# Attention over 16 heads on one core: one accumulation bank instead of two, four banks instead of three for the row maxima, one chunk per slot

## The chip, the cores and the metric

The kernel runs on one NeuronCore of a Trainium2 chip. The metric is the device time of one execution in microseconds (us), lower is better. The time given for a kernel is the median of its runs.

## The reference, cut to what matters

A macaron layer: half a gated feed-forward, causal attention, half a gated feed-forward, each on a layer norm of its input. 2048 tokens of width 512, 16 heads of width 32. Only the attention is touched here:

```python
scores = einsum('bhqd,bhkd->bhqk', q, k) / sqrt(32)
scores = scores + triu(full((S, S), -inf), k=1)      # S = 2048
attn = softmax(scores, axis=-1)
out = einsum('bhqk,bhkd->bhqd', attn, v)
return einsum('bsd,ed->bse', out, w_out) + b_out
```

All is float32, and the weights of the attention are scaled up, so the softmax needs its true row maximum.

## The kernel before

`build` (L1468) runs `ffn`, `attend`, `ffn`. `attend` runs `project_in` (queries, keys and values into DRAM; in its last steps also the row maxima of head 0), `attention`, and `project_out`. PSUM has 8 banks of 128 x 512 float32.

**Two sweeps over the scores of each head.** The first finds the row maxima, with queries on the partitions: a *chunk* (`max_chunk`, L705) is a matmul of 128 queries by up to 512 keys into one of the banks 4 to 6, and `take_max` (L729) on VectorE reduces it to one maximum a row; a chunk on the diagonal (L744) adds the mask in the same instruction. When the last chunk of a block of 512 queries is in, `split_max` (L748, three small VectorE instructions, L751, L756, L758) negates the maximum and splits it into a high and a low part. `rows` (L719) then transposes these with four small matmuls into a bank of the same ring, and `store_rows` (L761) on ScalarE copies the two rows into the query tile. The second sweep has keys on the partitions: `scores` (L1195) multiplies 98 rows, the last two being the maxima, into one of the banks 0 to 2; for a tile on the diagonal VectorE adds the mask of its first 128 columns (`mask`, L1250); `exps` (L1280) on ScalarE writes the exponential to SBUF; `with_values` (L1212) multiplies it by the values and a column of ones.

**Blocks, tiles, lanes.** A head has query blocks 0 to 3 with 4, 8, 12 and 16 key tiles: 40 tiles, and 40 chunks as well. The tiles (`TILES`, L583) alternate between two lanes, lane 0 with block 3 and then block 0 on output partitions 0 to 32, lane 1 with block 2 and then block 1 on partitions 64 to 96. A float32 matmul with values is two instructions, and those of the two lanes run at the same time. Blocks 3 and 2 are summed in bank 3, blocks 0 and 1 in bank 7 (`BANKS`, L592). Block 2's last tile is tile 23, block 3's is 30, block 0's 38 and block 1's 39. ScalarE copies a bank out (`take_out`, L1291) after tiles 30 and 39, and SyncE stores the copies.

**Slots, written out by hand.** A head is 40 slots, and each engine goes through them in program order. In slot t, `head` (L1226) on TensorE issues the scores of tile t + 4 (of the next head from slot 36 on), the chunks of the **next** head that `chunks_of_slot(t)` gives, and the row transposes if t is in `ROWS_AT`. After every fourth slot come the four `with_values` of these slots (a *batch*: slots 0 to 3 are batch 0, 36 to 39 batch 9). The chunks are packed into slots 0 to 35, with two in slots 0, 9, 18 and 27 and none in 36 to 39; maxima are split in slots 13, 24, 31 and 35, and transposed four slots later, in the middle or at the end of a batch. A chunk or transpose waits until its bank was emptied, three *items* earlier (`wait_for_max_bank`, L694); a score tile waits for the exponential three tiles earlier (L1204):

```python
ITEMS = [item for t in range(SLOTS)
         for item in [("chunk", m) for m in chunks_of_slot(t)] + ([("rows", ROWS_AT[t])] if t in ROWS_AT else [])]
```

The masked (diagonal) tiles are 4, 5, 10, 11, 16, 17, 22, 23 and 32 to 39, in the order of the slots. A loop body holds three heads and runs five times; head 15 comes after it, with no chunks. `wo_high` (L1316) is a large ScalarE copy just before head 15.

In `project_in`, `head_items_after` (L778) spreads the 44 items of head 0 over the last 17 of 32 steps, nine of them behind the last step.

Of the kernel before, what the change touches and what calls it, by code (L numbers as in the profile page):

```python
# [16 lines left out]
P = 128  # L17
# [597 lines left out]
MAX_BANKS = 3  # L615
DIAGONAL = [m for m in range(SLOTS) if CHUNKS[m][2] == CHUNKS[m][0]]


def max_bank_of(s, item):
    return (len(ITEMS) * s + ITEMS.index(item)) % MAX_BANKS  # L620


class Heads:
# [48 lines left out]
    def add_slot(self, nc, ctx):  # L672
        i = len(self.queries)
        self.queries.append(ctx.enter_context(nc.sbuf_tensor(f"queries{i}", [self.ROWS, TOKENS], F32R)))
        self.keys.append(ctx.enter_context(nc.sbuf_tensor(f"keys{i}", [self.ROWS, TOKENS], F32R)))
        self.values.append(ctx.enter_context(nc.sbuf_tensor(f"values{i}", [P, TT, VCOLS], F32)))
        ctx.enter_context(nc.sbuf_tensor(f"values_pad{i}", [P, TT, HD], F32))
# [16 lines left out]
    def wait_for_max_bank(self, pe, hp, s, item):  # L694

        before = len(ITEMS) * s + ITEMS.index(item) - MAX_BANKS
        if before < 0:
            return
        (kind, j), s = ITEMS[before % len(ITEMS)], before // len(ITEMS)
# [19 lines left out]
    def rows(self, pe, hp, s, b):  # L719

        pe.wait_ge(self.max_parts_ready, 12 * hp + (4 * s + RANK[b] + 1))
        self.wait_for_max_bank(pe, hp, s, ("rows", b))
# [55 lines left out]
def head_items_after(ep, s, tb):  # L778

    steps = 2 * KT * NTB - FIRST_MAXIMA  # L780
    i = 2 * NTB * ep + NTB * s + tb - FIRST_MAXIMA
    if i < 0:
        return []
    end = len(ITEMS) if i == steps - 1 else len(ITEMS) * (i + 1) // (steps + LEFT_TO_LAST)
    return ITEMS[len(ITEMS) * i // (steps + LEFT_TO_LAST):end]
# [337 lines left out]
def attention(nc, bank, o_heads, sums, inverses, w_out, b_out, heads, o):  # L1123
    with ExitStack() as ctx:
# [11 lines left out]
        start = sb("start", [P, 3], F32)  # L1136

        score_bank, out_bank = bank[0:SCORE_BANKS], [bank[3], bank[7]]
# [6 lines left out]
        out_stored = [sem(f"out_stored{i}") for i in range(2)]  # L1145
# [4 lines left out]
        def _(sp):  # L1150
            def store(h0, s, banks=range(2)):

                for e in banks:
                    sp.wait_ge(out_free, 2 * h0 + (2 * s + e + 1 + 2))
                    for lane in (1, 0):
                        b = BANKS[e][lane]
                        row = lane * LANE
                        sp.dma_start(o_heads[bass.ds(h0 * HD + s * HD, HD), cols(b, TB)],
                                     heads_out[row:row + HD, e, :]).then_inc(out_stored[e], 16)
                        sp.dma_start(sums[bass.ds(h0 + s, 1), cols(b, TB)],  # L1160
                                     heads_out[row + HD:row + VCOLS, e, :]).then_inc(out_stored[e], 16)
# [12 lines left out]
            for i in range(2):  # L1174
                sp.wait_ge(out_stored[i], 64 * (len(EARLY_HEADS) + 1))
# [7 lines left out]
            store(HEADS - 4, 3, [0])  # L1183
# [4 lines left out]
            store(HEADS - 4, 3, [1])  # L1188
            for i in range(2):
                sp.wait_ge(out_stored[i], 64 * (HEADS + 1))  # L1190

        @block.tensor
        def _(pe):

            def scores(hp, s, t, first=False):  # L1195

                b, kt = TILES[t]
                i = s % 3
                if t in FIRST_OF_BLOCK:
                    pe.wait_ge(heads.rows_ready, 12 * hp + (4 * s + RANK[b] + 1))  # L1200
                    if s == 2 and t == 0:
                        pe.wait_ge(heads.constants_ready, 7)
                if not (first and t < SCORE_BANKS):
                    pe.wait_ge(probs_ready, 120 * hp + (SLOTS * s + t - SCORE_BANKS + 1))  # L1204
                q0 = max(b * TB, kt * P)
                width = (b + 1) * TB - q0
                out = score_bank[(SLOTS * s + t) % SCORE_BANKS]
                pe.matmul(out[:, 0:width], keys[i][0:ROWS, cols(kt, P)], queries[i][0:ROWS, q0:q0 + width],  # L1208
                          start=True, stop=True, skip_group_check=True).then_inc(scores_ready, 1)

            def with_values(hp, s, t):
                b, kt = TILES[t]  # L1212
                i = s % 3
                if t in FIRST_OF_BLOCK:
                    pe.wait_ge(out_free, 6 * hp + (2 * s + BANK_OF[b] + 1))
                if t % BATCH == 0:
# [3 lines left out]
                last = pe.matmul(out_bank[BANK_OF[b]][row:row + VCOLS, off:TB], values[i][:, kt, :],  # L1220
                                 probs[:, t % RING, 0:TB - off], start=(t in FIRST_OF_BLOCK),
                                 stop=(t in LAST_OF_BLOCK), skip_group_check=True)
                if t in BANK_DONE:
                    last.then_inc(out_ready, 1)

            def head(hp, s, has_next):  # L1226
                for t in range(SLOTS):
                    if t + AHEAD < SLOTS:
                        scores(hp, s, t + AHEAD)
                    elif has_next:  # L1230
                        scores(hp, s + 1, t + AHEAD - SLOTS)
                    if has_next:
                        for m in chunks_of_slot(t):
                            heads.max_chunk(pe, hp, s + 1, m)
                        if t in ROWS_AT:
                            heads.rows(pe, hp, s + 1, ROWS_AT[t])
                    if t % BATCH == BATCH - 1:
                        for u in range(t + 1 - BATCH, t + 1):
                            with_values(hp, s, u)

            for t in range(AHEAD):
                scores(0, 0, t, first=True)
# [6 lines left out]
        def _(dve):  # L1249
            def mask(hp, s, t):  # L1250
                if t in DIAGONAL_TILES:
                    dve.wait_ge(scores_ready, 120 * hp + (SLOTS * s + t + 1))
                    square = score_bank[(SLOTS * s + t) % SCORE_BANKS][:, 0:P]
                    dve.tensor_tensor(square, square, heads.key_mask[:], ALU.add).then_inc(scores_masked, 1)  # L1254

            def head(hp, s, has_next):
                for t in range(SLOTS):
                    of, u = divmod(t + AHEAD, SLOTS)
                    if has_next or of == 0:
                        mask(hp, s + of, u)  # L1260
                    if has_next:
                        for m in chunks_of_slot(t):
                            heads.take_max(dve, hp, s + 1, m)
                        if t in MAXED_AT:
                            heads.split_max(dve, hp, s + 1, MAXED_AT[t])

            heads.fill_ones(dve, 2)
            for t in range(AHEAD):
                mask(0, 0, t)
# [9 lines left out]
        def _(act):  # L1279
            def exps(hp, s, t):  # L1280
                b, kt = TILES[t]
                width = TB - max(0, kt * P - b * TB)
                if t in DIAGONAL_TILES:
                    act.wait_ge(scores_masked, 48 * hp + (16 * s + DIAGONAL_TILES.index(t) + 1))
                else:
                    act.wait_ge(scores_ready, 120 * hp + (SLOTS * s + t + 1))
                source = score_bank[(SLOTS * s + t) % SCORE_BANKS][:, 0:width]
                act.activation(probs[:, t % RING, 0:width], source, ACT.Exp, scale=SM_SCALE)\  # L1288
                   .then_inc(probs_ready, 1)

            def take_out(hp, s, e):  # L1291
                act.wait_ge(out_ready, 6 * hp + (2 * s + e + 1))

                act.wait_ge(out_stored[e], 192 * hp + 64 * (s + 1))
                act.activation(heads_out[:, e, :], out_bank[e][0:LANE + VCOLS, :], ACT.Copy).then_inc(out_free, 1)
# [250 lines left out]
```

## Time and profile before

| | us |
|---|---|
| median of 3 runs | 3113.54 (3110.78 to 3115.54) |
| the profiled execution | 3114.36 |
| its span, first to last instruction | 3112.6 |
| PE busy, whole span | 2954.8 (95%) |
| DVE, ACT, POOL busy | 1898.8, 1062.3, 758.9 |
| mean granted TensorE clock | 0.977 of 2.4 GHz |

PE is TensorE's matmuls, PEld its weight loads, DVE is VectorE, ACT ScalarE, POOL GpSimd, SP SyncE. A matmul's duration runs from its start to the arrival of its last result, so matmuls overlap; what one costs is the distance from its start to the next one's start. "[x <-engine]" is the idle time before an instruction and what ended it. Times in rows of the timeline count from the start of the span.

### The profile page before, as it was taken

How to read it: one execution, taken by the hardware profiler on the slowest of the kernel's cores; microseconds unless marked ns; L12 is line 12 of the kernel's file. 1: busy time of each engine (PE TensorE's matmuls, PEld its weight loads, DVE VectorE, ACT ScalarE, POOL GpSimd, SP SyncE). 2: the span in 40 equal slices, each digit the busy share in tenths (PEclk: the TensorE clock that was granted, in tenths of full speed). 3: DMA queues.
4: the chain of work that ended last, by engine and by line, in shares of the span. 5: the costliest groups of instructions: out<-in, count | busy, mean ns of one | idle time of the engine just before them, and what ended most of it. 6: DMA issues, size and time to landing. Idle time of an engine off the chain costs nothing. (4 is left out here: it accounts for less than half of the span.)

```text
span 3112.6 us, 38714 instructions
## 1 busy us (share of the span) xinstructions
PE 2954.8 (95%) x12896; PEld 2193.4 (70%) x12896; DVE 1898.8 (61%) x3544; ACT 1062.3 (34%) x1781; POOL 758.9 (24%) x480
## 2 busy tenths in 40 slices
PE   5999999999999989999999996679999999999999
PEld 3788888888888858644444442458888888888887
DVE  7656655666556564677666662376655665656554
ACT  4322222222222232355555553142222222222222
POOL 4322222222222245200000001343222222222221
PEclk8999999999999989999999998889999999999999
DMA  3000000000000027522222221201000000000001
GB/s 95 21 28 28 24 23 20 27 26 21 27 20 20 1 64 185 151 55 55 55 54 55 55 52 37 87 14 32 23 27 20 27 21 27 27 20 21 26 14 55
DMA packets 120573, 127.61 MB, mean 41 GB/s; under 512 B 72672, under 2 KB 72928, under 8 KB 117152
## 3 DMA queue, kind: packets, MB, share of 16 engines
q1 hardware_dynamic: 119928, 125.93, 15.5%
q8 instruction: 41, 0.67, 0.1%
q10 hardware_dynamic: 552, 0.59, 0.1%
q14 instruction: 52, 0.43, 0.0%
HBM read 96.87 MB, written 29.62 MB: 41 GB/s over the span
## 5 line engine op out<-in xcount | busy, mean ns | idle before, releaser
L61 PE MATMUL psum<-ffn_x_high,ffn_w_high 128*128 128x512 f32 x2048 | 803.4, 392 | 17.1 <-DVE ffn_gelu L389 17.1
L62 PE MATMUL psum<-ffn_x_low,ffn_w_high 128*128 128x512 f32 x2048 | 798.5, 390 | 0.0
L63 PE MATMUL psum<-ffn_x_high,ffn_w_low 128*128 128x512 f32 x2048 | 798.5, 390 | 0.0
L526 POOL TENSOR_TENSOR ffn_inner<-ffn_gelu,ffn_inner 128x512 fp32r<-128x512 f32 x256 | 346.0, 1352 | 1156.7 <-ACT ffn_inner L471 1156.7
L379 DVE SCALAR_TENSOR_TENSOR ffn_gelu<-ffn_gelu,psum 128x512 f32<-128x512 f32 x256 | 175.9, 687 | 599.8 <-ACT ffn_gelu L464 599.7
L61 PEld LDWEIGHTS psum<-ffn_x_high,ffn_w_high 128*128 128x128 f32 x2048 | 386.0, 188 | 101.9 <-DVE ffn_gelu L389 20.2
L62 PEld LDWEIGHTS psum<-ffn_x_low,ffn_w_high 128*128 128x128 f32 x2048 | 385.8, 188 | 82.2 <-issue 2.3
L63 PEld LDWEIGHTS psum<-ffn_x_high,ffn_w_low 128*128 128x128 f32 x2048 | 385.5, 188 | 80.7
L61 PE MATMUL psum<-ffn_inner,ffn_w_high 128*128 128x512 f32 x1024 | 398.6, 389 | 0.2
L62 PE MATMUL psum<-ffn_inner,ffn_w_high 128*128 128x512 f32 x1024 | 398.4, 389 | 0.0
L63 PE MATMUL psum<-ffn_inner,ffn_w_low 128*128 128x512 f32 x1024 | 398.3, 389 | 0.0
L1288 ACT ACTIVATE probs<-psum 128x512 f32<-128x512 f32 (+3 forms) x640 | 310.6, 534 | 243.2 <-DVE psum L1254 125.9
L464 ACT ACTIVATE ffn_gelu<-psum 128x512 f32<-128x512 f32 x256 | 152.7, 597 | 531.6 <-PE psum L63 531.6
L395 DVE SCALAR_TENSOR_TENSOR x<-psum,x 128x512 f32<-128x512 f32 x512 | 320.9, 681 | 16.2 <-PE psum L63 16.2
L520 POOL TENSOR_TENSOR ffn_w_low<-ffn_weight,ffn_w_high 128x1024 fp32r<-128x1024 f32 x96 | 232.3, 2420 | 329.2 <-ACT ffn_w_high L457 329.2
L471 ACT ACTIVATE ffn_inner<-ffn_gelu 128x512 fp32r<-128x512 f32 x256 | 161.9, 633 | 381.0 <-DVE ffn_gelu L389 381.0
L736 DVE TENSOR_REDUCE chunk_max<-psum 128x1 f32<-128x512 f32 x384 | 254.9, 685 | 55.8 <-PE psum L714 55.8
L383 DVE SCALAR_TENSOR_TENSOR ffn_gelu<-ffn_gelu,psum 128x512 f32<-128x512 f32 x256 | 175.9, 687 | 179.9 <-ACT ffn_gelu L466 179.9
L1220 PE MATMUL psum<-probs,values 128*33 128x512 f32 (+3 forms) x1280 | 268.1, 540 | 0.0
L1208 PE MATMUL psum<-queries,keys 98*128 98x512 f32 (+3 forms) x640 | 246.6, 408 | 12.4 <-ACT probs L1288 11.1
L714 PE MATMUL psum<-keys,queries 96*128 96x512 f32 (+3 forms) x640 | 240.1, 393 | 14.5 <-DVE chunk_max L736 12.5
L457 ACT ACTIVATE ffn_w_high<-ffn_weight 128x1024 fp32r<-128x1024 f32 x96 | 101.9, 1062 | 402.1 <-DVE ffn_weight L370 402.1
(112 smaller groups left out, 3064.8 us busy)
## 6 DMA issues: line engine op xcount, KB each, us to landing
ffn_words<-packed SPq DMA_DIRECT2D x96, 256.0 KB
ffn_word_scales<-scales SPq DMA_DIRECT2D x96, 256.0 KB
qk_parts<-parts SPq DMA_DIRECT2D x32, 512.0 KB, 4.0
queries<-qk_parts SPq DMA_DIRECT2D x48, 256.0 KB, 4.0
keys<-qk_parts SPq DMA_DIRECT2D x48, 256.0 KB, 6.1
x<-x_in SPq DMA_DIRECT2D x4, 1024.0 KB, 13.7
v_parts<-parts SPq DMA_DIRECT2D x16, 256.0 KB, 4.6
values<-v_parts SPq DMA_DIRECT2D x16, 256.0 KB, 7.7
```

The lines of the kernel that those rows point to most:

```text
L61: pe.matmul(out, w_high, x_high, start=first, stop=False, skip_group_check=True)
L62: pe.matmul(out, w_high, x_low, start=False, stop=False, skip_group_check=True)
L63: return pe.matmul(out, w_low, x_high, start=False, stop=last, skip_group_check=True)
L379: dve.scalar_tensor_tensor(out=cubic[m], in0=square[m], scalar=1.0 / GELU_A, in1=gate_bank[m], op0=ALU.add, op1=ALU.mult)\
L395: dve.scalar_tensor_tensor(out=x[:, k, cols(tb, TB)], in0=down_bank[k], scalar=FFN_BACK, in1=x[:, k, cols(tb, TB)], op0=ALU.mult, op1=ALU. ...
L520: pool.tensor_tensor(w_low[s][:, :, piece, :], weight[:, q % 2, :, :], f32(w_high[s][:, :, piece, :]), ALU.subtract).then_inc(w_low_ready, 1)
L526: pool.tensor_tensor(inner[:, tb % 2, m, 1, :], product[m], f32(inner[:, tb % 2, m, 0, :]), ALU.subtract)\
L714: last = pe.matmul(out[:, 0:width], self.queries[i][0:self.STACK, cols(qt, P)], self.keys[i][0:self.STACK, c * TB:c * TB + width], start=T ...
L736: dve.tensor_reduce(chunk_max, scores, AX.X, ALU.max).then_inc(self.max_taken, 1)
L1208: pe.matmul(out[:, 0:width], keys[i][0:ROWS, cols(kt, P)], queries[i][0:ROWS, q0:q0 + width], start=True, stop=True, skip_group_check=True ...
L1220: last = pe.matmul(out_bank[BANK_OF[b]][row:row + VCOLS, off:TB], values[i][:, kt, :], probs[:, t % RING, 0:TB - off], start=(t in FIRST_O ...
L1288: act.activation(probs[:, t % RING, 0:width], source, ACT.Exp, scale=SM_SCALE)\
```

## The change

Four things. (1) All sums over the values go to bank 3. Block 1 follows block 2 on its partitions, block 0 follows block 3, so there are three copies a head: block 2 after tile 23 (33 partitions), block 3 after tile 30 (33 partitions), blocks 1 and 0 after tile 39 (97). (2) Bank 7 joins the ring of the maxima, four banks. (3) One chunk a slot: chunk t in slot t. The maxima of blocks 3, 2, 1, 0 are thus split at slots 15, 27, 35 and 39. The transposes stand first in a batch: block 3's at slot 16, block 2's at 32, block 1's at slot 0 and block 0's at slot 8 **of the head itself**. (4) Within a batch the score tiles are issued unmasked first (`ORDER`), e.g. 6, 7, 4, 5. The ring of exponentials grows from 8 to 12 tiles, and one padding tile of SBUF goes.

```diff
-BANKS = [(3, 2), (0, 1)]
-BANK_OF = {b: e for e, pair in enumerate(BANKS) for b in pair}
-BANK_DONE = [max(t for t in range(SLOTS) if BANK_OF[TILES[t][0]] == e) for e in range(2)]
+OUTS = [(2,), (3,), (1, 0)]
+OUT_DONE = [max(t for t in range(SLOTS) if TILES[t][0] in blocks) for blocks in OUTS]
+
+OUTS_BEFORE = {3: 0, 2: 0, 1: 1, 0: 2}
 SCORE_BANKS = 3
 BATCH = 4
-AHEAD = 4
-RING = AHEAD + BATCH
+AHEAD = BATCH
+RING = 3 * BATCH
...
-ROWS_AFTER = 4
-def chunks_of_slot(t):
-    return [m for m in range(SLOTS) if m * (SLOTS - ROWS_AFTER) // SLOTS == t]
-MAXED_AT = {[t for t in range(SLOTS) if LAST_CHUNK[b] in chunks_of_slot(t)][0]: b for b in BLOCKS}
-ROWS_AT = {t + ROWS_AFTER: b for t, b in MAXED_AT.items()}
+ORDER = [t for j in range(0, SLOTS, BATCH)
+         for t in sorted(range(j, j + BATCH), key=lambda t: (t in DIAGONAL_TILES, t not in DIAGONAL_TILES and t % 2, t))]
+ROWS_AT = {0: 1, 8: 0, 16: 3, 32: 2}
+OWN_ROWS = (1, 0)
 ITEMS = [item for t in range(SLOTS)
-         for item in [("chunk", m) for m in chunks_of_slot(t)] + ([("rows", ROWS_AT[t])] if t in ROWS_AT else [])]
-MAX_BANKS = 3
+         for item in ([("rows", ROWS_AT[t])] if t in ROWS_AT else []) + [("chunk", t)]]
+ITEMS_BEFORE = [item for item in ITEMS if item[0] == "chunk" or item[1] not in OWN_ROWS]
+MAX_BANKS = 4
...
 def with_values(hp, s, t):
...
     if t in FIRST_OF_BLOCK:
-        pe.wait_ge(out_free, 6 * hp + (2 * s + BANK_OF[b] + 1))
+        pe.wait_ge(out_free, 9 * hp + (3 * s + OUTS_BEFORE[b] + 3))
...
 def head(hp, s, has_next):              # TensorE
     for t in range(SLOTS):
-        if t + AHEAD < SLOTS:
-            scores(hp, s, t + AHEAD)
-        elif has_next:
-            scores(hp, s + 1, t + AHEAD - SLOTS)
+        if t in ROWS_AT and (has_next or ROWS_AT[t] in OWN_ROWS):
+            heads.rows(pe, hp, s + (ROWS_AT[t] not in OWN_ROWS), ROWS_AT[t],
+                       alone=not has_next)
+        of, u = divmod(t + AHEAD, SLOTS)
+        if has_next or of == 0:
+            scores(hp, s + of, u)
         if has_next:
-            for m in chunks_of_slot(t):
-                heads.max_chunk(pe, hp, s + 1, m)
-            if t in ROWS_AT:
-                heads.rows(pe, hp, s + 1, ROWS_AT[t])
+            heads.max_chunk(pe, hp, s + 1, t)
         if t % BATCH == BATCH - 1:
...
 def head(hp, s, has_next):              # ScalarE
     for t in range(SLOTS):
-        if t + AHEAD < SLOTS:
-            exps(hp, s, t + AHEAD)
-        elif has_next:
-            exps(hp, s + 1, t + AHEAD - SLOTS)
-        if has_next and t in ROWS_AT:
-            heads.store_rows(act, hp, s + 1, ROWS_AT[t])
+        if t in ROWS_AT and (has_next or ROWS_AT[t] in OWN_ROWS):
+            heads.store_rows(act, hp, s + (ROWS_AT[t] not in OWN_ROWS), ROWS_AT[t])
+        of, u = divmod(t + AHEAD, SLOTS)
+        if has_next or of == 0:
+            exps(hp, s + of, u)
         if t % BATCH == BATCH - 1:
-            for e in range(2):
-                if t - BATCH < BANK_DONE[e] <= t:
+            for e in range(len(OUTS)):
+                if t - BATCH < OUT_DONE[e] <= t:
                     take_out(hp, s, e)
```

SyncE stores the three copies one by one with the same eight DMAs a head, and the loads of a later head still follow the last of them. In `project_in` the items of head 0 are 42, without the transposes of blocks 1 and 0; again nine follow the last step.

## Rows read from the trace of the kernel before

**Rows 1.** One head as a window: length, busy PE, PEld, DVE, ACT, POOL, clock, DMA, GB/s.

```profile
1501.65:1540.80 39.15, 37.85 (x178) 17.96 (x176) 27.30 (x100) 22.88 (x46) 0.00 (x0) 1.00 0.29 56
```

**Rows 2.** Waits between 1300 and 1880 us: total us, times, longest.

```profile
PEld psum L714 <- DVE chunk_max L736: 46.0, 103, 1.1
```

**Rows 3.** Timeline of PE: with_values of batches 2 to 9, 0 and 2.

```profile
1500.24 1.49 PE L1220 MATMUL psum<-probs,values 128*33 128x512 f32 x8
...
1503.67 1.91 PE L1220 MATMUL psum<-probs,values 128*33 128x512 f32 x8
...
1508.22 1.70 PE L1220 MATMUL psum<-probs,values 128*33 128x384 f32 x8
...
1511.85 1.91 PE L1220 MATMUL psum<-probs,values 128*33 128x512 f32 x8
...
1516.85 1.91 PE L1220 MATMUL psum<-probs,values 128*33 128x512 f32 x8
...
1521.25 1.91 PE L1220 MATMUL psum<-probs,values 128*33 128x512 f32 x8
...
1525.07 1.70 PE L1220 MATMUL psum<-probs,values 128*33 128x512 f32 x8
...
1528.56 0.84 PE L1220 MATMUL psum<-probs,values 128*33 128x256 f32 x8
...
1531.83 1.91 PE L1220 MATMUL psum<-probs,values 128*33 128x512 f32 x8
...
1539.39 1.49 PE L1220 MATMUL psum<-probs,values 128*33 128x512 f32 x8
```

**Rows 4.** Timeline of PE: batch 5, and the wait and a transpose in batches 6 and 7.

```profile
1509.85 0.49 PE L1208 MATMUL psum<-queries,keys 98*128 98x512 f32 x1
1510.18 0.40 PE L714 MATMUL psum<-keys,queries 96*128 96x512 f32 x1
1510.42 0.40 PE L1208 MATMUL psum<-queries,keys 98*128 98x512 f32 x1
...
1516.53 0.39 PE L714 MATMUL psum<-keys,queries 96*128 96x256 f32 x1 [0.81 <-DVE chunk_max L736]
...
1519.26 0.40 PE L724 MATMUL psum<-ident_r,max_parts 128*2 128x128 f32 x4
1519.50 0.44 PE L1208 MATMUL psum<-queries,keys 98*128 98x512 f32 x1
```

**Rows 5.** Timeline of DVE in batch 3, to the end of the split.

```profile
1502.13 0.30 DVE L1254 TENSOR_TENSOR psum<-psum,key_mask 128x128 f32<-128x128 f32 x1 [0.70 <-PE psum L1208]
1502.37 0.69 DVE L736 TENSOR_REDUCE chunk_max<-psum 128x1 f32<-128x512 f32 x1
1502.97 0.29 DVE L1254 TENSOR_TENSOR psum<-psum,key_mask 128x128 f32<-128x128 f32 x1
1503.18 0.68 DVE L744 CUSTOM_DVE_ANT_0 masked<-psum,query_mask 128x512 f32<-128x512 f32 x1
...
1504.40 0.16 DVE L758 TENSOR_TENSOR max_parts<-minus_max,max_parts 128x4 fp32r<-128x4 f32 x1
```

**Rows 6.** Timeline of ACT: exponentials, a store of rows and a copy out.

```profile
1527.24 2.06 ACT L1288 ACTIVATE probs<-psum 128x512 f32<-128x512 f32 x4 [0.81 <-PE psum L1208]
1529.33 0.58 ACT L764 ACTIVATE queries<-psum 2x512 fp32r<-2x512 f32 x1
1529.94 0.60 ACT L1295 ACTIVATE heads_out<-psum 97x512 f32<-97x512 f32 x1
```

**Rows 7.** Timeline of PE at the end of project_in and the start of attention.

```profile
1288.21 0.40 PE L724 MATMUL psum<-ident_r,max_parts 128*2 128x128 f32 x4 [1.21 <-DVE max_parts L758]
...
1289.81 1.62 PE L1208 MATMUL psum<-queries,keys 98*128 98x512 f32 x3 [1.20 <-PEq L789]
```

**Rows 8.** Timeline of PE at the start of the last head.

```profile
1884.46 0.50 PE L1208 MATMUL psum<-queries,keys 98*128 98x512 f32 x1 [2.50 <-ACT probs L1288]
```

**Rows 9.** A window at the start of attention, columns as in rows 1.

```profile
1290.00:1295.00 5.00, 4.71 (x12) 3.31 (x13) 3.89 (x7) 3.53 (x8) 0.13 (x2) 0.50 0.85 205
```

More of the change, by code:

```diff
@@ L1134, in attention @@
         heads_out = sb("heads_out", [LANE + VCOLS, 2, TB], F32)
[L1136 to L1138 removed]
+        start = sb("start", [P, 4], F32)
+        score_bank, out_bank = bank[0:SCORE_BANKS], bank[SCORE_BANKS]
         scores_ready = sem("scores_ready")
@@ L1187, in _, with score_bank_of, scores @@
                     load_inverse(sp, o, inverses, tb, k, o.early_loaded[tb])
-            store(HEADS - 4, 3, [1])
-            for i in range(2):
-                sp.wait_ge(out_stored[i], 64 * (HEADS + 1))
+            store(HEADS - 4, 3, [2])
+            wait_for_stores(HEADS)
         @block.tensor
         def _(pe):
-            def scores(hp, s, t, first=False):
-                b, kt = TILES[t]
+            def score_bank_of(s, u):
+                return score_bank[(SLOTS * s + u) % SCORE_BANKS]
+            def scores(hp, s, u, first=False):
+                b, kt = TILES[ORDER[u]]
                 i = s % 3
-                if t in FIRST_OF_BLOCK:
+                if u in FIRST_SCORE:
                     pe.wait_ge(heads.rows_ready, 12 * hp + (4 * s + RANK[b] + 1))
-                    if s == 2 and t == 0:
+                    if s == 2 and u == 0:
                         pe.wait_ge(heads.constants_ready, 7)
-                if not (first and t < SCORE_BANKS):
-                    pe.wait_ge(probs_ready, 120 * hp + (SLOTS * s + t - SCORE_BANKS + 1))
+                if not (first and u < SCORE_BANKS):
+                    pe.wait_ge(probs_ready, 120 * hp + (SLOTS * s + u - SCORE_BANKS + 1))
                 q0 = max(b * TB, kt * P)
                 width = (b + 1) * TB - q0
-                out = score_bank[(SLOTS * s + t) % SCORE_BANKS]
-                pe.matmul(out[:, 0:width], keys[i][0:ROWS, cols(kt, P)], queries[i][0:ROWS, q0:q0 + width],
-                          start=True, stop=True, skip_group_check=True).then_inc(scores_ready, 1)
+                pe.matmul(score_bank_of(s, u)[:, 0:width], keys[i][0:ROWS, cols(kt, P)],
+                          queries[i][0:ROWS, q0:q0 + width], start=True, stop=True,
+                          skip_group_check=True).then_inc(scores_ready, 1)
             def with_values(hp, s, t):
@@ L1219, in with_values @@
                 row = t % 2 * LANE
-                last = pe.matmul(out_bank[BANK_OF[b]][row:row + VCOLS, off:TB], values[i][:, kt, :],
-                                 probs[:, t % RING, 0:TB - off], start=(t in FIRST_OF_BLOCK),
+                last = pe.matmul(out_bank[row:row + VCOLS, off:TB], values[i][:, kt, :],
+                                 probs[:, (SLOTS * s + t) % RING, 0:TB - off], start=(t in FIRST_OF_BLOCK),
                                  stop=(t in LAST_OF_BLOCK), skip_group_check=True)
-                if t in BANK_DONE:
+                if t in OUT_DONE:
                     last.then_inc(out_ready, 1)
@@ L1261, in head @@
                     if has_next:
[L1262 to L1265, printed above, removed]
+                        heads.take_max(dve, hp, s + 1, m)
+                        if m == LAST_CHUNK[CHUNKS[m][0]]:
+                            heads.split_max(dve, hp, s + 1, CHUNKS[m][0])
             heads.fill_ones(dve, 2)
-            for t in range(AHEAD):
-                mask(0, 0, t)
+            for u in range(AHEAD):
+                mask(0, 0, u)
             with dve.Fori(0, HEADS // 3) as hp:
@@ L1320, in _ @@
         def _(pool):
-            pool.memset(start[:, 0:1], 0.0).then_inc(out_free, 2)
-            pool.memset(start[:, 1:2], 0.0).then_inc(out_stored[0], 64)
-            pool.memset(start[:, 2:3], 0.0).then_inc(out_stored[1], 64)
+            pool.memset(start[:, 0:1], 0.0).then_inc(out_free, 3)
+            for e in range(len(OUTS)):
+                pool.memset(start[:, e + 1:e + 2], 0.0).then_inc(out_stored[e], 32 * len(OUTS[e]))
             pool.wait_ge(o.wo_high_ready, 1)
@@ L1460, in attend @@
     with ExitStack() as ctx:
-        heads = Heads(nc, ctx, bank[4:7], qk_parts, v_parts)
+        heads = Heads(nc, ctx, bank[4:8], qk_parts, v_parts)
         project_in(nc, x, bank, w_v, b_v, w_qk, b_qk, qk_parts, v_parts, heads)
```

101 lines of the change are left out of this document (60 added, 41 removed).

## The prediction

> **What bounds the kernel now.** I read the timeline's windows first, then the waits, then PE's own timeline over one head. Outside the attention nothing is changed, so the question is what one head costs. A head lasts 39.15 us, PE is busy for 37.85 of them at clock 1.00, DVE for 27.30 and ACT for 22.88 [rows 1]. That busy share hides waits: matmuls overlap, so a late one looks like a long one. PE is the bound, and what counts is from start to start.
>
> The waits say what holds it: weight loads of the chunks waited 46.0 us for VectorE's reductions over some 15 heads, most of it under a running matmul [rows 2]. To place this I cut the head into its ten batches. Each with_values group ends 0.07 us after the next batch's first score starts (1508.22 + 1.70 = 1509.92 against 1509.85) [rows 3, 4], which dates every boundary. Batches 3 to 8 last 3.86, 4.34, 3.84, 5.00, 4.40 and 3.61 us, batch 9 2.63, batch 0 4.35, batches 1 and 2 together 7.12; the sum is 39.15 [rows 3]. Batches 5 and 6 have the same eight values matmuls, and batch 6 is 1.16 us longer: the second chunk of slot 27 sat idle 0.81 us for a reduction, as VectorE had split a maximum just before, with only three banks to run ahead in [rows 4].
>
> **Prices.** Batch 5 shows a batch without waits: score to first chunk 0.33, then 0.23 to 0.24 a matmul of 512 columns [rows 4], 2.00 us from the first score (1509.85) to the values (1511.85), which hold PE 1.84 to the next score [rows 3]. I call the two parts front and values. A transpose (four matmuls) costs 0.24 [rows 4]. VectorE passes a 512 column reduction every 0.60 (1502.37 to 1502.97), a mask in 0.21, and a diagonal chunk of 512 with its split ends 1.38 after the chunk's start (1503.18 to 1504.56) [rows 5]. An exponential follows the last every 0.49 (three steps and a last 0.60 are 2.06), a row store or a copy takes 0.61 of ScalarE [rows 6]. The first exponential of a batch starts 0.53 after its score, and the fourth score needs that exponential finished: 0.53 + 0.60 + 0.06, about 1.2 after the first score (1527.24 less 0.54 is batch 9's start at 1526.70), while in a full batch it comes at 1.5 anyway [rows 3, 4, 6].
>
> **Part by part.**
>
> *One chunk a slot and a fourth bank.* The double slots go, and a chunk waits for the chunk four items earlier, in the batch before. VectorE needs at most 4 x 0.60 plus two masks and a split, 2.4 + 0.4 + 0.7 = 3.5 us, in a batch of 3.7 to 3.8 [rows 5], so I see no chunk wait left. Batch 6 becomes a front of 1.99 (one chunk is 384 wide) and 1.84: 3.83, a gain of 1.17. Batch 7 loses a transpose (moved) and its small chunk waits, but keeps four masked scores: first exponential 0.87 instead of 0.53 after the score, so the fourth score comes at 1.54, the values at 2.10; 3.94, a gain of 0.46. Batches 3 and 5 have nothing to lose but cents: 3.77 and 3.83, together 0.10. Batch 8 now carries wider chunks, and the transpose of block 2 first: values at 2.07, then 1.63, 3.70, a loss of 0.09. Batch 9 takes four chunks (128, 256, 384 and 512 wide) where PE waited for the exponentials before; front 1.88, values 0.77, 2.65, a loss of 0.02. That cover, about half a microsecond of PE's idle time in slots 36 to 39, is what makes moving them there free; without it they would cost 1280 columns, 0.6 us.
>
> *Transposes first in a batch.* Four of 0.24 each, as before; no row shows one right behind the values, where a first matmul is 0.1 dearer for its follower. Bounds: 0.14 (the transpose takes that drain over from the score) and 0.55; I take 0.24, the nearest row's. Block 3's has a new wait. Its maxima are split after chunk 15, in slot 15, and it stands at the head of slot 16. By the prices above VectorE in batch 3 runs: reductions at 0.77 and 1.37 after the batch's start, mask 1.98, reduction 2.19, mask 2.80, diagonal chunk 3.01, split done 4.40; now it is done at 1504.56, which is 2.91 after 1501.65, and two more reductions come ahead of it [rows 3, 5]. PE gets there at 3.77 and starts 0.05 after the split: **a stall of 0.70 us a head**, with every score, chunk and value of the next batch queued behind it. Bounds: 0.4 (masks falling better) and 1.1. Batch 4 is 0.70 + 0.24 + a front of 1.93 + values of 1.63 = 4.50, against 4.34, a loss of 0.16. Blocks 2, 1 and 0 have four, four and eight slots to spare (split at 27, 35 and 39): a wait of nothing.
>
> On ScalarE the row store now stands ahead of the batch's exponentials. It is ready 0.44 after the transpose starts, the first exponential 0.61 later at 1.05, the fourth score not before 1.71; PE gets there at 1.74. Hidden in batches 2 and 4. In batch 0 the copy out comes before it as well (ready at 0.15, store 0.75, exponential 1.36, fourth score 2.02): front 2.47, 4.32 against 4.35.
>
> *Batches 1 and 2.* 3.05 + 3.66 = 6.71 against 7.12: the masked tiles last, no double slot 9, the transpose (0.24) in; a gain of 0.41.
>
> *One bank for the sums.* One copy more a head, 0.61 of ScalarE [rows 6]. It falls behind the exponentials of slot 27 and delays batch 6's first one by 0.23; the fourth score could come at 1.42 and is issued at 1.50. The cover is ScalarE's idle time (16 of 39 us [rows 1]); gone, it would be 0.61 a head. Block 1's first product, at slot 27, needs that copy: it ends 0.8 into batch 6, the values start at 2.0. Blocks 0 and the next head's block 3 likewise have over 1.2 us. Values of both lanes keep their pace in one bank: batches 3 (one bank) and 6 (two) both show 1.91 [rows 3]. SyncE's eight stores and the seven loads behind them keep their place after the last copy; a load is needed two heads later, 78 us. A fourth start memset on GpSimd and the longer ring cost nothing: the first is needed 30 us on, the second adds no wait.
>
> **Sum of a head.** 1.17 + 0.46 + 0.10 - 0.09 - 0.02 - 0.16 + 0.03 + 0.41 = 1.90 us, 37.25 instead of 39.15. Fifteen heads: 28.5 us.
>
> *Ends.* In `project_in` the last transpose waited for VectorE, and the attention began 1.60 after it (1288.21 to 1289.81) [rows 7]. Now VectorE has one reduction more behind the last step (0.60) and nobody transposes or stores: 0.5 us gained. The last head has no chunks, so ScalarE paces it: its two own transposes bring row stores in front of exponentials, 0.5 us each, the extra copy 0.2, masks last give 0.2 back: 1.0 lost; the wait of 2.50 us for the large copy ahead of it [rows 8] stays. Altogether 28.5 + 0.5 - 1.0 = 28.0. The profiled execution took 3114.4, 0.8 above the median 3113.5, so I forecast 3086.4 on its scale and **3085.5** on the median's.
>
> **Rivals.**
>
> *A. The forecast:* waits gone, a stall of 0.7 us at slot 16; 0.72.
>
> *B. The moves cost more than they save in small things:* transposes behind the values at 0.55 instead of 0.24 (1.2 a head) or row stores holding the fourth score in four batches. For it: the switch from values to scores is PE's dearest in [rows 4] (0.33 before the chunk). Against: 0.24 in the only place seen. 0.7 us a head remain: 3103. Chance 0.10.
>
> *C. The stall is nearly hidden* because VectorE's order falls better, and the 0.14 transposes hold: 0.3 + 0.4 more a head; 3075. Chance 0.08.
>
> *D. The change doesn't do what it says:* the chunk waits were VectorE's rate, not the banks, and come back in batches 3 to 8. For it: 27.3 busy us of 39.15 and dense batches. Against: it has 12 us of slack a head [rows 1]. Gain under 0.2 a head: 3111. Chance 0.05.
>
> *E. Slower:* the new gap comes 15 times, right behind values that use 33 of 128 columns, and TensorE falls to half clock there. Attention's start shows the low level, 0.50 of 2.4 GHz [rows 9]. If it fell once a head, one batch's front and values of 3.8 us would run twice as long: 15 x 3.8 = 57 lost, 28 gained, 3142. It decides once the gap takes the clock below 1.00; against it, a gap of 0.81 a head (1516.53) in a head at clock 1.00 throughout [rows 1, 4]. Chance 0.05.
>
> The Trainium skill, TensorE: Matmul & The Clock Gate, section "A second HAM failure mode: psum-queue depth-cycling", says that a kernel which cycles through banks of PSUM and idles briefly between groups makes the clock swing between its levels. By that rule E is the outcome; the trace disagrees so far, as the head with the 0.81 us gap ran at 1.00.
>
> **How the numbers follow.** Two in ten may stay out: E and the far side of D. The bounds of a head are 1.0 us (transposes dear, stall 1.1) and 2.7 (stall 0.4, transposes 0.14, batch 7 without its mask wait): 3099 to 3073. Widened by the 2 us between runs, and upward to rival B: 3072 to 3101. A measurement tells 0.2%, about 6 us, from no change. A, B and C are faster by more (0.90, and a little of D), D mostly within, E slower: 0.91, 0.05, 0.04.
>
> **What would show it.** Right: a head of 37.2 us; no idle of 0.8 before a chunk; the transpose at slot 16 idle about 0.7 for the split, the other three not waiting; batch 6 at 3.8 and batch 4 at 4.5. Wrong: chunks still waiting for reductions, a transpose followed by a gap, a clock below 1.00 inside the loop, or values waiting for a copy out.

## The result and the profile after

| | before | after |
|---|---|---|
| median, us | 3113.54 (3110.78 to 3115.54, 5 runs) | 3099.48 (3097.15 to 3099.73, 5 runs) |
| ratio, 95% interval | | 0.9953, 0.9939 to 0.9968 |
| profiled execution | 3114.36 | 3097.15 |
| its span | 3112.6 | 3095.3 |

Both medians are of five runs. The change gains 14.1 us by the medians, half of the forecast 28.0, and 17.2 us between the two profiled executions (the one after is the fastest of its five). Nearly all of it lies in the attention: from its first score to the start of its last product it takes 610.2 us (1288.96 to 1899.18) instead of 626.3 (1289.81 to 1916.13), and it starts 0.85 us earlier.

Windows of the kernel after, columns as in [rows 1]: an ordinary head, 550 us of the loop, and a head that starts a pass of the loop.

```profile
1483.92:1521.60 37.68, 36.38 (x179) 17.86 (x177) 27.42 (x102) 23.49 (x47) 0.00 (x0) 1.00 0.29 56
1330.00:1880.00 550.00, 525.47 (x2528) 255.05 (x2529) 387.87 (x1421) 340.51 (x681) 4.51 (x1) 1.00 0.27 54
1407.40:1446.10 38.70, 36.89 (x178) 17.66 (x176) 27.27 (x101) 23.33 (x47) 0.00 (x0) 1.00 0.29 55
```

A head of 39.15 us has become one of 37.68, but every third one still takes 38.7 to 39.0 (the last window ends 0.08 us before its head does). The clock stays at 1.00 in these windows. The waits of the kernel after, 1300 to 1860 us (us in total, times, longest):

```profile
ACT probs L1309 <- DVE psum L1276: 101.0, 166, 2.8
DVE chunk_max L755 <- PE psum L730: 80.9, 80, 1.6
...
PEld psum L1230 <- ACT probs L1309: 68.3, 140, 0.9
...
ACT queries L783 <- PE psum L743: 20.3, 15, 1.4
...
DVE chunk_max L755 <- issue: 11.6, 4, 3.1
...
PE psum L743 <- DVE max_parts L777: 9.6, 15, 0.6
```

The 46.0 us in which chunks waited for VectorE [rows 2] have no line any more. Two lines are new: the transpose that waits for the split (15 times, 9.6 us of idle PE), and a reduction on VectorE that waits for nothing the profile shows ("issue"), four times, up to 3.1 us. The with_values groups of the ordinary head, which answer to [rows 3]:

```profile
1486.36 1.91 PE L1243 MATMUL psum<-probs,values 128*33 128x512 f32 x8
...
1489.92 1.27 PE L1243 MATMUL psum<-probs,values 128*33 128x128 f32 x8
...
1493.57 1.49 PE L1243 MATMUL psum<-probs,values 128*33 128x512 f32 x8
...
1496.93 1.91 PE L1243 MATMUL psum<-probs,values 128*33 128x512 f32 x8
...
1501.83 1.70 PE L1243 MATMUL psum<-probs,values 128*33 128x384 f32 x8
...
1505.40 1.91 PE L1243 MATMUL psum<-probs,values 128*33 128x512 f32 x8
...
1509.36 1.91 PE L1243 MATMUL psum<-probs,values 128*33 128x512 f32 x8
...
1513.21 1.91 PE L1243 MATMUL psum<-probs,values 128*33 128x512 f32 x8
...
1517.35 1.70 PE L1243 MATMUL psum<-probs,values 128*33 128x512 f32 x8
...
1520.82 0.84 PE L1243 MATMUL psum<-probs,values 128*33 128x256 f32 x8
```

Cut in the same way over heads 1 to 14, a batch (front and values) takes on average, in us. A stall of the transpose ahead of batch 4 counts to batch 3 here, since it comes before batch 4's first instruction:

| batch | 0 | 1 | 2 | 3 | 4 | 5 | 6 | 7 | 8 | 9 | head |
|---|---|---|---|---|---|---|---|---|---|---|---|
| before | 4.28 | 3.15 | 3.96 | 3.87 | 4.34 | 3.86 | 5.00 | 4.40 | 3.60 | 2.63 | 39.09 |
| forecast | 4.32 | 3.05 | 3.66 | 4.47 | 3.80 | 3.83 | 3.83 | 3.94 | 3.70 | 2.65 | 37.25 |
| after | 4.29 | 3.26 | 3.82 | 4.50 | 3.99 | 3.80 | 3.97 | 3.85 | 3.93 | 2.62 | 38.02 |

The transpose of block 3, and what VectorE did before it:

```profile
1499.47 0.40 PE L743 MATMUL psum<-ident_r,max_parts 128*2 128x128 f32 x4 [0.63 <-DVE max_parts L777]
...
1501.16 0.50 PE L1230 MATMUL psum<-queries,keys 98*128 98x512 f32 x1
1501.50 0.40 PE L730 MATMUL psum<-keys,queries 96*128 96x512 f32 x1
```

```profile
1497.15 0.68 DVE L755 TENSOR_REDUCE chunk_max<-psum 128x1 f32<-128x512 f32 x1
1497.75 0.29 DVE L1276 TENSOR_TENSOR psum<-psum,key_mask 128x128 f32<-128x128 f32 x1
1497.95 0.69 DVE L763 CUSTOM_DVE_ANT_0 masked<-psum,query_mask 128x512 f32<-128x512 f32 x1
...
1499.18 0.16 DVE L777 TENSOR_TENSOR max_parts<-minus_max,max_parts 128x4 fp32r<-128x4 f32 x1
```

The split ends at 1499.34, the transpose starts 0.13 later, 4.49 us after batch 3 began at 1494.98, where the forecast had 4.45. Behind it, the fourth score of batch 4 starts at 1501.16, 0.21 after a chunk of 128 columns, which elsewhere costs 0.07 (1481.63 to 1481.70), and the next chunk only 0.34 later. ScalarE shows why:

```profile
1499.91 0.58 ACT L783 ACTIVATE queries<-psum 2x512 fp32r<-2x512 f32 x1 [1.34 <-PE psum L743]
1500.51 1.08 ACT L1309 ACTIVATE probs<-psum 128x512 f32<-128x512 f32 x2
```

The row store goes first, the first exponential ends at 1501.11, and the score that needs its bank starts at 1501.16.

Last, VectorE where its loop over the heads begins its next pass:

```profile
1407.95 0.16 DVE L777 TENSOR_TENSOR max_parts<-minus_max,max_parts 128x4 fp32r<-128x4 f32 x1
1410.99 1.29 DVE L755 TENSOR_REDUCE chunk_max<-psum 128x1 f32<-128x512 f32 x2 [2.87 <-issue]
```

Its chunk was in the bank long before (the first of that head started at 1407.92). The other three passes begin with a pause of 2.8 to 3.1 us as well. Before the change VectorE's first instruction there was the mask of a score that was not computed yet, behind slots without chunks. It came 2.88 to 2.90 us after the last in the heads inside a pass, and 2.90 to 3.07 in those that start one: a pause of VectorE's own cost next to nothing there. What VectorE does in it is not shown. In each of the four pauses of the kernel after, a DMA packet of kind "instruction" (8 KB) starts 0.9 us after VectorE's last instruction; whose instructions it carries the trace does not say.

### The profile page after: what moved, and what is told of

Read it like the earlier page. It is cut to its first block and busy times, and to the rows that moved or that the text cites. A ratio compares the mean times of both kernels' runs of the same rounds, so it can differ in the third digit from the quotient of the medians.

```text
span 3095.3 us, 38774 instructions
## 1 busy us (share of the span) xinstructions
PE 2935.3 (95%) x12896; PEld 2193.4 (71%) x12896; DVE 1900.3 (61%) x3544; ACT 1071.8 (35%) x1797; POOL 759.3 (25%) x481
## 5 line engine op out<-in xcount | busy, mean ns | idle before, releaser
L1230 PE MATMUL psum<-queries,keys 98*128 98x512 f32 (+3 forms) x640 | 253.9, 409 | 21.2 <-ACT probs L1309 17.6
L730 PE MATMUL psum<-keys,queries 96*128 96x512 f32 (+3 forms) x640 | 228.5, 370 | 1.6 <-ACT queries L783 1.2
```

The costliest lines, as they stand in the source:

```text
L730: last = pe.matmul(out[:, 0:width], self.queries[i][0:self.STACK, cols(qt, P)], self.keys[i][0:self.STACK, c * TB:c * TB + width], start=T ...
L1230: pe.matmul(score_bank_of(s, u)[:, 0:width], keys[i][0:ROWS, cols(kt, P)], queries[i][0:ROWS, q0:q0 + width], start=True, stop=True, skip_ ...
```

## The experiments

Every kernel was compared with the kernel before on its own chip. "A head" is again the mean of heads 1 to 14, "ordinary" a head that does not start a pass of the loop (3, 6, 9 and 12 start one), from the starts of TensorE's instructions in each trace. The first four test the stall, the loop, the banks and the row store one at a time, on the changed kernel.

**Block 3's transpose at slot 20.**

```diff
-ROWS_AT = {0: 1, 8: 0, 16: 3, 32: 2}
+ROWS_AT = {0: 1, 8: 0, 20: 3, 32: 2}
```

> The changed kernel with block 3's transpose at slot 20 instead of 16. Theory: in the changed kernel VectorE ends the split 4.5 us after the start of batch 3 and PE waits for it about 0.71 us in every one of 15 heads, and nothing else holds PE there. With four slots in between the wait goes: 15 x 0.71 = 10.6 us, less about 0.1 a head because the row store now stands ahead of batch 5's exponentials: 3089 to 3091 (the changed kernel had a median of 3099.5). Rival: the wait only covers another one (ScalarE's exponentials or VectorE's backlog), and half or more comes back in batches 4 and 5: 3094 or more.

Measured: 3088.78 us, ratio 0.9922 (0.9905 to 0.9938). A head is 37.34 us, 0.69 less than in the changed kernel: batches 3 and 4 fall from 4.50 + 3.99 to 3.79 + 3.58, and batch 5, which now has the transpose and the row store, rises from 3.80 to 4.20. The theory holds to 0.2 us. The stall was a plain loss with nothing under it: 15 x 0.69 = 10.3 of the 10.7 us gained.

**VectorE's loop written out.**

```diff
-            with dve.Fori(0, HEADS // 3) as hp:
+            for hp in range(HEADS // 3):
```

> The changed kernel with VectorE's loop over the heads written out (the other engines keep theirs). Theory: VectorE idles 3 us at the start of each pass of its loop (4 passes after the first); before the change it waited there for a mask anyway, now a reduction is due, and batch 1 of every third head is 1.1 to 1.3 us longer than of the others (front 2.88 against 1.72). Without the loop its front is 1.7 in all heads and 4 to 5 us are gained: 3094 to 3096. Rival: VectorE fetches straight-line code as slowly as a loop's start, and the idle time appears elsewhere: 3098 to 3101.

Measured: 3090.53 us, 0.9934 (0.9917 to 0.9951), 9 us less than the changed kernel by the medians, though the intervals overlap and one of the four runs took 3097.73. It is more than either theory gave. The front of batch 1 is 1.73 in every head, and VectorE's reductions wait for TensorE only:

```profile
its engine sat idle before it (us, times) until:
  PE psum L730: 94.1, 91
```

Heads 3, 6, 9 and 12 give 4 x 1.1 us, as expected. The stall before batch 4 is 0.09 shorter in each head (values part 2.46 instead of 2.55), 1.4 us in all; why VectorE ends the split sooner without the loop was not tried by itself. Another 1.7 us lie in the head after the loop: its batches 0 to 7 take 29.69 instead of 31.35 us. These cannot be credited to the loop. In both kernels TensorE waits there 2.90 us for ScalarE; after it the clock falls to 0.50 for 3.4 us in the changed kernel and stays at 1.00 in this one. The changed kernel first, then this one:

```profile
1868.18 0.33 PE L1230 MATMUL psum<-queries,keys 98*128 98x128 f32 x1 [2.90 <-ACT probs L1309]
1868.43 3.32 PE L1243 MATMUL psum<-probs,values 128*33 128x512 f32 x8
```

```profile
1862.69 0.33 PE L1230 MATMUL psum<-queries,keys 98*128 98x128 f32 x1 [2.90 <-ACT probs L1309]
1862.94 1.91 PE L1243 MATMUL psum<-probs,values 128*33 128x512 f32 x8
```

**Three banks for the maxima.**

```diff
-MAX_BANKS = 4
+MAX_BANKS = 3
```

> The changed kernel with three banks in the ring of the maxima (bank 7 unused), one chunk a slot kept. Theory: the even spread of the chunks does most of the work in batches 6 and 7, and three banks cost only where a row store sits in the ring (batches 0 and 8) and behind the split: 0.3 to 0.6 us a head, 3104 to 3108. Rival: the fourth bank is what took the 0.81 us wait away, and without it batch 6 is near 5 us again: 3114 or more.

Measured: 3110.29 us, 0.9992 (0.9982 to 1.0002). Both theories miss. The ordinary heads take 37.7 us, as with four banks (37.68 to 37.78, against 37.66 to 37.76), with batch 6 at 3.97: where the chunks are spread evenly, the fourth bank does nothing for a head as a whole (without it batch 1 is 0.11 longer and batch 2 0.10 shorter). The heads that start a pass take 41.5 to 42.8 us instead of 38.7 to 39.0. There TensorE runs out of banks in VectorE's pause:

```profile
1409.40 0.33 PE L1230 MATMUL psum<-queries,keys 98*128 98x128 f32 x1
1411.84 0.33 PE L730 MATMUL psum<-keys,queries 96*128 96x128 f32 x1 [2.11 <-DVE chunk_max L755]
1412.10 2.44 PE L1243 MATMUL psum<-probs,values 128*33 128x512 f32 x8
1414.47 0.79 PE L1230 MATMUL psum<-queries,keys 98*128 98x512 f32 x1
```

and the clock falls at the gap, as it does in the other three passes (window of that kernel, columns as in [rows 1]):

```profile
1413.40:1416.80 3.40, 3.40 (x10) 1.95 (x7) 1.11 (x5) 1.47 (x3) 0.00 (x0) 0.51 1.01 224
```

**The row store behind the first exponential.**

```diff
-                    if t in ROWS_AT and (has_next or ROWS_AT[t] in OWN_ROWS):
-                        heads.store_rows(...)
                     of, u = divmod(t + AHEAD, SLOTS)
                     if has_next or of == 0:
                         exps(hp, s + of, u)
+                    if t in ROWS_AT and (has_next or ROWS_AT[t] in OWN_ROWS):
+                        heads.store_rows(...)
```

> The changed kernel with the row store behind the first exponential of its batch on ScalarE instead of ahead of it. Theory: in batches 0, 2, 4 and 8 the fourth score waits for a first exponential that the row store holds up by 0.3 to 0.6 us, and the matmul behind the wait is another 0.1 late; the sum of 1.1 to 1.4 us a head goes: 16 to 20 us, 3080 to 3084. Rival: the exponentials of these batches are late for another reason (masks, copies out), or the late store now holds the chunk that reuses the bank: 3094 or more.

Measured: 3098.26 us, 0.9952 (0.9935 to 0.9968), no change against the changed kernel. The theory is refuted, and the second half of the rival holds. The score's wait is gone in batch 4 of this kernel, and the chunk behind it waits instead:

```profile
1500.95 0.58 ACT L783 ACTIVATE queries<-psum 2x512 fp32r<-2x512 f32 x1
```

```profile
1501.12 0.44 PE L1230 MATMUL psum<-queries,keys 98*128 98x512 f32 x1
1501.58 0.49 PE L730 MATMUL psum<-keys,queries 96*128 96x512 f32 x1
```

The store ends at 1501.53, and the chunk four items after the transpose, which needs that bank, starts at 1501.58. Fronts of batches 0, 2, 4 and 8: 2.24, 2.35, 2.41 and 2.42, against 2.44, 2.40, 2.36 and 2.30. With the transpose first in a batch, the row store stands in somebody's way in both places tried.

**The transposes last in a batch.** They go behind the chunk of slots 3, 11, 19 and 35, the row stores behind the batch's last exponential.

```diff
-ROWS_AT = {0: 1, 8: 0, 16: 3, 32: 2}
+ROWS_AT = {3: 1, 11: 0, 19: 3, 35: 2}
...
-         for item in ([("rows", ROWS_AT[t])] if t in ROWS_AT else []) + [("chunk", t)]]
+         for item in [("chunk", t)] + ([("rows", ROWS_AT[t])] if t in ROWS_AT else [])]
```

> The changed kernel with the four transposes last in a batch (slots 3, 11, 19 and 35, behind the chunk and ahead of the values) and the row stores behind the last exponential of the batch. Theory: the row store is what holds the fourth score (first in the batch) or the chunk that takes its bank again (behind the first exponential); under the values nothing waits for it, and the split of block 3 has four slots more. So the 0.71 us stall goes and the fronts of batches 0, 2, 4 and 8 fall from 2.44, 2.40, 2.36 and 2.30 to 2.2, 2.2, 2.1 and 2.1: 0.7 + 0.9 = 1.6 us a head, 24 us, 3073 to 3078. Rival: only the stall goes, since ScalarE's exponentials set these fronts: 3087 to 3091, as with the transpose at slot 20.

Measured: 3081.13 us, 0.9895 (0.9879 to 0.9912). Ordinary heads take 35.9 us, 1.8 less than in the changed kernel and more than the theory gave: fronts of batches 0, 2, 4 and 8 are 1.95, 2.26, 2.19 and 1.98. But the heads that start a pass now take 38.6 to 40.3 us, since a transpose closes their batch 0, the fifth item in a ring of four, and it waits for a bank through VectorE's whole pause:

```profile
1405.31 0.58 PE L744 MATMUL psum<-ident_r,max_parts 128*2 128x128 f32 x4 [2.58 <-DVE chunk_max L756]
1405.83 3.35 PE L1244 MATMUL psum<-probs,values 128*33 128x512 f32 x8
```

```profile
1405.30:1408.70 3.40, 3.39 (x12) 0.86 (x12) 1.76 (x7) 1.14 (x3) 0.00 (x0) 0.51 1.03 243
```

The same eight matmuls take 1.91 us in the other heads; here they run at 0.51 of the clock. The third pass has a gap of 2.54 us too, but there the clock stays at 1.00 and the head takes the 38.6 us; the three passes with a fall take 40.2 to 40.3. The whole kernel, at 3081.13 us, is therefore slower than the theory's window, though its ordinary heads are faster.

**The same with VectorE's loop written out.**

> The same with VectorE's loop written out. Theory: the two gains add, as they lie in different batches: another 7 to 9 us, 3065 to 3070. Rival: with the transposes last, batch 0 and 1 have slack for VectorE's late start, and it adds less than 4: 3070 or more.

Measured: 3065.20 us, 0.9840 (0.9823 to 0.9856), the best of all. Every head takes 35.8 to 35.9 us; 15.9 us come from the loop alone, above the theory's 7 to 9, as the three falls of the clock at its passes go too.

**Three banks with VectorE's loop written out.**

> The changed kernel with three banks for the maxima and VectorE's loop written out. Theory: with three banks the heads that do not start a pass of the loop lasted 37.7 us, as with four; the fourth bank only covers part of VectorE's late start. Without that start three banks are as good as four: 3089 to 3092 (four banks: 3090.5). Rival: the banks matter by themselves: 3096 or more.

Measured: 3095.13 us, 0.9941 (0.9924 to 0.9957). A head takes 37.65 us, with four banks 37.64: in the loop the theory holds to the hundredth. The median is 3 us above its window, and 4.6 above the one with four banks; the profiled executions differ by 1.9 in span (3089.2 and 3087.3), of which the last head, 31.02 against 29.69, is the larger part: here the clock fell there, with four banks it did not. The intervals overlap, so for the whole kernel the two are not told apart.

The last group asks the opposite: the old, packed placement of chunks and transposes, with the new banks and the new order of masked tiles.

**Packed chunks, four banks.** `chunks_of_slot`, `MAXED_AT` and `ROWS_AT` as before the change, all transposes for the next head, no `OWN_ROWS`; one bank for the sums stays.

> The changed kernel with the chunks packed into slots 0 to 35 and the transposes four slots behind their split, as before the change; one bank for the sums, four for the maxima and the new order of the masked tiles stay. Theory: a fourth bank is worth something only where chunks are packed: the wait of 0.81 us in batch 6 goes nearly all, batches 3 to 7 lose their small waits, no stall at slot 16, and VectorE's late start falls into slots without chunks: 37.3 to 37.9 us a head, 3085 to 3096. Rival: packing itself costs, VectorE falls behind in batches 6 and 7 whatever the banks: 38.5 or more a head, 3104 or more.

Measured: 3080.34 us, 0.9888 (0.9871 to 0.9904). A head takes 36.71 us, below the theory's 37.3 to 37.9, and 1.3 less than in the changed kernel; no head stands out.

**Packed chunks, three banks.** The same with `MAX_BANKS = 3`.

> The packed chunks of e9 with three banks for the maxima: against the kernel before this changes only the order of the masked tiles and the one bank for the sums. Theory: the wait of batch 6 comes back (5.0 us instead of 4.08), the small waits of batches 0, 3, 4 and 7 too; the new order saves up to 0.5 a head: 38.6 to 39.0 us a head, 3106 to 3113. Rival: the gain of e9 (3080) came from the order of the masked tiles, and stays: 3095 or less.

Measured: 3114.83 us, 1.0004 (0.9995 to 1.0014), with 39.13 us a head and batch 6 at 5.00. One bank for the sums and the order of the masked tiles are worth nothing here; between three and four banks lie 34 us. The time is 2 us above the theory's window: the order saves nothing.

**The changed kernel with tiles in the order of their slots.**

```diff
-ORDER = [t for j in range(0, SLOTS, BATCH)
-         for t in sorted(range(j, j + BATCH), key=lambda t: (t in DIAGONAL_TILES, t not in DIAGONAL_TILES and t % 2, t))]
+ORDER = list(range(SLOTS))
```

> The changed kernel with the score tiles in the order of their slots, as before the change. Theory: in batches 0, 1 and 3 (with masked tiles first among four) the exponentials wait for a mask and the fourth score waits for them; 0.1 to 0.2 us each, 0.3 to 0.6 a head: 3104 to 3109. Rival: the order is worth nothing where the row store comes first anyway: 3098 to 3101.

Measured: 3102.67 us, 0.9965 (0.9951 to 0.9979), between the two windows. The ordinary heads are *shorter*, 37.3 us, and the stall is 0.38 instead of 0.71 (values part of batch 3 at 2.22): the masks of batch 3 come first, as in [rows 5], and no longer between VectorE's last reductions. The heads that start a pass are longer, 39.9 to 42.7: with a masked tile first, the fourth score waits behind VectorE's pause (TensorE idle for 2.56 to 2.72 us), and the clock falls at three of the four gaps. The interval overlaps that of the changed kernel.

**Packed chunks, four banks, slot order.** Against the kernel before only the banks differ: four for the maxima, one for the sums with its three copies (and the ring of exponentials).

> The packed chunks of e9 with four banks and the tiles in the order of their slots: against the kernel before only the banks are changed. Theory: the fourth bank does nearly all, 1.5 to 2.0 us a head, and the order 0.4 to 0.6: 3085 to 3091. Rival: bank and order need each other, and alone each gives under 1 us a head: 3100 or more.

Measured: 3076.34 us, 0.9879 (0.9862 to 0.9895): better than the theory's window, with 36.59 us a head. The new order is no help here (36.71 with it, and the two intervals overlap). A reading of the fronts for the two packed kernels and the changed one, in us:

| front of batch | 0 | 1 | 2 | 3 | 4 | 5 | 6 | 7 | 8 | 9 |
|---|---|---|---|---|---|---|---|---|---|---|
| before | 2.43 | 1.95 | 2.55 | 2.02 | 2.72 | 2.01 | 3.16 | 2.56 | 1.98 | 1.86 |
| packed, four banks, slot order | 2.08 | 1.74 | 2.25 | 2.02 | 2.36 | 2.01 | 2.24 | 2.19 | 1.98 | 1.86 |
| packed, four banks | 2.28 | 1.74 | 2.24 | 1.95 | 2.35 | 2.01 | 2.24 | 2.20 | 1.98 | 1.86 |
| changed | 2.44 | 2.06 | 2.40 | 1.95 | 2.36 | 1.96 | 2.13 | 2.01 | 2.30 | 1.85 |
| transposes last, no loop on VectorE | 1.95 | 1.73 | 2.26 | 1.96 | 2.19 | 1.96 | 2.13 | 2.01 | 1.98 | 1.85 |

**The best version in slot order.**

> The best so far (transposes last, VectorE's loop written out, 3065.2) with the score tiles in the order of their slots. Theory: the order pays only where the row store or the split is late; with both out of the way it moves a head by under 0.2 us either way (batch 3 about 0.07 longer, batch 0 up to 0.2 shorter): 3062 to 3068. Rival: the slot order is better by itself, as with packed chunks (36.59 against 36.71 a head and 3076 against 3080): 3061 or less.

Measured: 3066.80 us, 0.9850 (0.9834 to 0.9867), as the theory had it: with the late steps out of the way the order does nothing that can be measured.

## Why the prediction was right, and where it was half wrong

The sign and the mechanism held, and the measured time lies in the range, but only 1.5 us inside its slow end and nearer to rival B's 3103 than to the forecast: the chunk waits went, batch 6 shrank by 1.03 us (forecast 1.17), batch 7 by 0.55 (0.46), batch 9 took four chunks for nothing (2.62 against 2.63). The stall at slot 16, a wait that no row of before contained, was forecast at 0.70 and was 0.71; that it can be taken away whole is shown. Batches 0, 3, 5 and 9 came out within 0.03. Rival C (the stall nearly hidden) and rival D (waits from VectorE's rate) are out, and E did not occur in the loop of this kernel. Half of rival B did: the transposes cost the forecast 0.24 (1483.92 to 1484.16, first in a batch), but the row stores did hold the fourth score.

The size was off by a factor of two: a head saved 1.07 us instead of 1.90. What makes the missing 0.83 us, and then the ends:

- **A term that was absent: VectorE's loop.** The step that VectorE needs at most 3.5 us in a batch of 3.7 to 3.8, "so I see no chunk wait left", counted instructions and left out the pause of 3 us before the first instruction of each pass. Moving chunks into slots 36 to 39 took away the idle time that had covered it. In heads 1 to 14 it is 4 x 1.1 us, 0.3 a head. Written out, the loop gives 9 us by the medians: 4.4 of them lie in these four heads and 1.4 in the stall, and 1.7 go with a clock that happened not to fall in the last head. That the pause is the loop's is shown best with the transposes last, where writing it out gives 15.9 us and the intervals lie apart.
- **Row stores ahead of exponentials, undersized.** The forecast called them hidden in batches 2 and 4, and used the same 1.74 for the fourth score in both. In batch 4 the third chunk has only 128 columns, so that score is due at 1.57 after the transposes' start, not 1.74, and the 1.71 of the exponential is what holds. The matmul after a waiting one was also another 0.10 late (1501.16 to 1501.50), which no term had. Batches 2, 4 and 8 are 0.16, 0.19 and 0.23 longer than forecast; the experiment with the transposes last takes 0.14, 0.17 and 0.32 off these fronts, and 0.49 off batch 0. Storing one exponential later moved the wait from the score to the chunk and gave nothing.
- **The copy of block 2**, priced at nothing, delays batch 6's first exponential to 0.81 after the score and costs 0.14. These three make 1.0 us a head; batch 1 (2.92 in ordinary heads, forecast 3.05) and batch 7 give 0.2 back.
- **The ends:** 0.5 us forecast and 0.9 measured at the start of attention; the last head, forecast 1.0 longer, is the same (31.35 against 31.36 for its batches 0 to 7). That it is the same is luck: after the wait for ScalarE's large copy the clock was at 0.50 for 6.8 us before the change and for 3.4 us after it. The front of the head's batch 0 did grow, from 3.65 to 4.13 us; with the transposes last it is 3.63.

What the prediction had wrong beside the size is the credit. It gave the gain to "one chunk a slot and a fourth bank" as one edit. They are two cures for one wait: spread chunks need no fourth bank in an ordinary head (37.7 with three or four), and packed chunks with a fourth bank need no spreading (36.6). In the changed kernel the second adds nothing, and what came along with the spreading, transposes first in a batch and chunks in the last slots, gives 1.3 us a head back against the packed kernel: the split too late for slot 16, row stores in front, the loop's pause uncovered. The spreading is not worthless for that: with the transposes last and VectorE's loop written out it takes 35.87 us a head against 36.59 packed, and 3065.20 against 3076.34 us, with intervals that lie apart. Which of the differences between these two kernels brings the 0.7 us was not tried alone.

Rival E named the right point and the wrong place. The clock of the changed kernel stays at 1.00 through a gap of 0.63 us a head. At longer gaps of TensorE it fell to 0.50 in most cases, not in all: at ten of the twelve gaps of 1.91 to 2.72 us where a pass of the loop starts (three banks, slot order, transposes last), and at the gap of 2.09 to 2.90 us in the last head in twelve of the fourteen kernels. A gap of 2.54 us and one of 2.90 left the clock at 1.00, so its length alone does not decide; what does stays open. The Trainium skill (TensorE: Matmul & The Clock Gate, "A second HAM failure mode: psum-queue depth-cycling") speaks of micro-idle, frequent enough, between groups of matmuls in a kernel that cycles through banks; here the short gaps, once a head, did nothing, and the prediction had left the "frequent" out.

## What to carry to other kernels

Before moving work into idle slots, ask on each engine what the idle time was covering; a loop's next pass is such a thing, and it shows in a trace only once nothing else hides it. A deeper ring and an even schedule may cure the same wait: try each alone, and begin with the one that moves nothing else; the other paid here only after what it had moved was put right. A short instruction for a later stage (here a row store) belongs where its engine's next result is not waited for: last in a batch nothing was seen to wait for it, first it held a score, second a chunk.

## What the runs showed that was not expected

- VectorE's first instruction of a loop's pass came 2.8 to 3.1 us after the last of the pass before, in all four passes, with its data ready; written out as straight code, it had no such pause (0.3 us, for TensorE, at the same place).
- Gaps of 1.9 to 2.9 us in TensorE's work, in the loop and in the last head, came with a granted clock of 0.50 for 3.4 to 6.8 us in 22 of 26 cases; gaps of 0.63 or 0.81 us did not. The same gap of 2.90 us came with a fall in one kernel and not in another, and the difference in time, 1.7 us, is easily taken for the work of an edit.
- A fourth bank with the old schedule is worth 34 us (3114.83 to 3080.34, both with the new order of tiles), and the bank is free because the sums over the values run as fast in one bank as in two (values parts of 1.84 us in both).
- The best kernel, transposes last and VectorE's loop written out, takes 3065.20 us, 48 us less than the kernel before.
